# Full attention: the rows of maxima are sent from ScalarE's queue instead of SP's

## The reference, cut to what matters

```
xn  = layernorm(x)                                   # x: 16 x 512 x 256
out = x + full_attention(xn) + two_layers(xn)

full_attention(xn):                                  # 16 heads of 16
    q, k, v = split(xn @ w_qkv.T);  q, k = rope(q), rope(k)
    scores  = q @ k.T / sqrt(16)                     # per head 512 x 512
    out     = softmax(scores) @ v;  return out @ w_out.T
```

## Time and profile before

| | |
|---|---|
| median of 3 runs | 4582.62 us (4575.4 to 4592.76) |
| the profiled execution | 4582.86 us |
| its span | 4581.1 us, 78049 instructions |
| PE busy | 3692.3 us, 81% |
| DVE busy | 2838.8 us, 62% |
| ACT busy | 2356.2 us, 51% |
| POOL busy | 1516.8 us, 33% |
| granted TensorE clock, mean | 0.926 of full speed |
| DMAs of the rows of maxima | 128, 2.0 KB each, from SP |
| stacking DMAs | 384, 64.0 KB each, from SP |

### The profile page before, as it was taken

One profiled execution on the slowest core, in us unless ns is written; L12 is line 12 of the kernel. 1 busy time (PEld: TensorE's weight loads), 2 busy tenths in 40 slices (PEclk: granted clock), 3 DMA queues, 4 the chain that ended last, 5 costly groups with the idle time before them and its releaser, 6 DMA issues.

```text
span 4581.1 us, 78049 instructions
## 1 busy us (share of the span) xinstructions
PE 3692.3 (81%) x28256; PEld 2044.9 (45%) x28256; DVE 2838.8 (62%) x4578; ACT 2356.2 (51%) x2874; POOL 1516.8 (33%) x1468
## 2 busy tenths in 40 slices
PE   3787778777846888888888888666888888888888
PEld 1222222222224555555555555444555555555555
DVE  5676767676734666656666566345566665666664
ACT  1555455555533555555555655334655556555564
POOL 1101111011022434444434444134444344443452
PEclk8999999899967999999999999787999999999999
DMA  2212121212110001000000000200000000000000
GB/s 44 47 38 46 38 47 37 47 37 46 33 62 17 22 21 32 21 21 30 21 27 25 21 30 16 74 17 12 21 30 21 27 26 21 30 21 26 27 21 21
DMA packets 149334, 139.48 MB, mean 30 GB/s; under 512 B 11421, under 2 KB 147665, under 8 KB 149201
## 3 DMA queue, kind: packets, MB, share of 16 engines
q1 hardware_dynamic: 149200, 137.78, 12.0%
HBM read 70.40 MB, written 33.55 MB: 23 GB/s over the span
## 4 chain that ended last, share of the span: by engine, by line
PE 35%; issue 13%; DVE 10%; POOL 9%; ACT 5%; SPq 0%; DMA 0%; POOLq 0%; DVEq 0%; ACTq 0%
PE f_p L950 10%; PE f_p L1056 5%; PE f_p L1020 4%; POOL f_u L1409 4%; POOL f_hT_l L1421 3%; PE f_p L1078 2%; PE f_p L1031 2%; PE f_p L1002 2%; DVE f_negm L1290 2%; DVE f_rt L245 2%; PE f_p L1039 1%; POOL f_qst L1415 1%; PE f_p L934 1%; PE f_p L1046 1%; PE f_p L1006 1%
## 5 line engine op out<-in xcount | busy, mean ns | idle before, releaser
L646 DVE TENSOR_REDUCE m_negm<-m_p 128x2 f16<-128x1024 f32 x512 | 604.9, 1221 | 244.7 <-PE m_p L465 200.7
L565 ACT ACTIVATE m_Pr<-m_p 128x1024 f32<-128x1024 f32 x512 | 492.4, 1018 | 264.6 <-PE m_p L483 264.0
L1404 POOL TENSOR_TENSOR f_u<-f_u,f_bt 128x1024 f32<-128x1024 f32 x128 | 301.5, 2356 | 903.1 <-DVE f_bt L1262 903.1
L1290 DVE TENSOR_REDUCE f_negm<-f_p 128x4 bf16<-128x1024 f32 x256 | 293.5, 1223 | 194.8 <-PE f_p L973 194.5
L685 POOL TENSOR_TENSOR m_rc<-m_rc,m_rs 128x1024 f32<-128x1024 f32 x32 | 75.5, 2359 | 979.6 <-DVE m_rs L641 978.0
L492 PE MATMUL m_o<-m_Pr,m_vm 128*32 128x512 f32 x2048 | 368.1, 672 | 17.2 <-ACT m_Pr L565 16.6
L963 PE MATMUL f_p<-f_ident,f_qst 128*128 128x128 f16 x1024 | 97.3, 251 | 309.8 <-POOL f_qst L1415 309.8
L1421 POOL TENSOR_TENSOR f_hT_l<-f_hp,f_hT_h 128x512 f16<-128x512 f32 x192 | 235.6, 1227 | 308.2 <-ACT f_hp L1184 307.5
L1285 DVE TENSOR_TENSOR f_klt<-f_u,f_khh 128x512 f16<-128x512 f32 x128 | 135.4, 1058 | 317.9 <-ACT f_khh L1131 317.9
L1078 PE MATMUL f_p<-f_xhT_h,f_w_h 128*128 128x512 f16 (+1 forms) x768 | 302.7, 394 | 0.0
L1078 PE MATMUL f_p<-f_xhT_h,f_w_l 128*128 128x512 f16 (+1 forms) x768 | 300.9, 392 | 0.0
(11 more groups left out here) (225 smaller groups left out, 8965.4 us busy)
## 6 DMA issues: line engine op xcount, KB each, us to landing
f_xs<-out SPq DMA_DIRECT2D x32, 512.0 KB, 4.2
f_xr<-out SPq DMA_DIRECT2D x32, 512.0 KB, 3.9
f_ar<-attn_res SPq DMA_DIRECT2D x32, 512.0 KB, 4.4
out<-f_xb SPq DMA_DIRECT2D x32, 512.0 KB, 3.2
m_xin<-in_L_attn_x SPq DMA_DIRECT2D x16, 512.0 KB, 4.3
m_QT<-m_hi SPq DMA_DIRECT2D x128, 64.0 KB
m_KT<-m_hi SPq DMA_DIRECT2D x128, 64.0 KB
out<-m_xn SPq DMA_DIRECT2D x16, 512.0 KB, 6.5
```

Of the source, the lines that this page charges most:

```text
L565: act.activation(Pr[kt % 2][:, 2 * u:2 * u + 2, :].rearrange("p h t -> p (h t)"), psum[w.slot("M2", g, kt, u)][:, :], ACT.Exp).then_inc(*w ...
L646: dve.tensor_reduce(negm[:, t, pr // 2, :, pr % 2], psum[w.slot("M1", h, u)][:, :].rearrange("p (a k) -> p a k", a=2), AX.X, ALU.max, nega ...
L1290: dve.tensor_reduce(negm[:, :, h], psum[w.slot("L1", h)][:, :].rearrange("p (n k) -> p n k", n=NT), AX.X, ALU.max, negate=True).then_inc(* ...
L1404: pool.tensor_tensor(u[t][:], u[t][:], bt[:], ALU.add).then_inc(*bt_used.up(I))
```

## The change

What does not change: the arithmetic, the tiles, the order of TensorE, VectorE and GpSimd, and the places of the four MM steps in ScalarE's list. What changes is who issues the 128 DMAs of the rows and where the other steps of SP stand because of it. In ScalarE's step `mmax`, behind the copy, ScalarE now waits until its own copy has completed (`is_drained`) and issues the two DMAs. The step `mmax` of SP is gone, and so are its four words in SP's list. SP's list begins with two more quotes, so that its first word reads `""B.MM,0`; that stream isn't given, and the word is dropped.

```diff
-        "SP": """B.MM,0 A.LX T.MP B.MM,1 B.MM,2 A.ST,0 A.ST,1 A.ST,2 A.ST,3 A.ST,4 A.ST,5 B.MM,3 A.ST,6 A.ST,7 A.LS""",
+        "SP": """""B.MM,0 A.LX T.MP A.ST,0 A.ST,1 A.ST,2 A.ST,3 A.ST,4 A.ST,5 A.ST,6 A.ST,7 A.LS""",
...
                 act.wait_ge(*mrow_done.at(I, 32 * g))
                 act.activation(mT[:], psum[w.slot("MM", g)][:, :].bitcast(F16)[0:HG, 0:T], ACT.Copy)\
                     .then_inc(*w.frees("MM", g))
+                act.wait_ge(*w.is_drained("MM", g))
+                for e in range(2):
+                    act.dma_start(QT[I.par][e * S + KR:e * S + KR + 1, g * HG // 2:(g + 1) * HG // 2, :],
+                                  mT[e * HG // 2:(e + 1) * HG // 2, :]).then_inc(*mrow_done.up(I, 16))
...
-            def mmax(I, g):
-                hold(w.is_drained("MM", g))
-                for e in range(2):
-                    sp.dma_start(QT[I.par][e * S + KR:e * S + KR + 1, g * HG // 2:(g + 1) * HG // 2, :],
-                                 mT[e * HG // 2:(e + 1) * HG // 2, :]).then_inc(*mrow_done.up(I, 16))
-
...
-            w.run({"LX": lx, "LS": ls, "ST": stack, "MM": mmax, "MP": mp})
+            w.run({"LX": lx, "LS": ls, "ST": stack, "MP": mp})
```

## The result

The kernel after takes 4651.6 us (median of 4 runs, 4645.8 to 4655.6), the one before 4585.2 (4 runs): ratio 1.0145, 95% interval 1.0122 to 1.0168. That is 66 us slower. I had forecast 41, and the time lies 6 us above the range. The profiled execution has a span of 4651.6 us, 70.5 above that of before.

A forecast was written before the change was run, and what follows sets the result against it. A once-per-batch loop through the stacking DMAs' transfers and ScalarE's Exps was taken to bound the attention phase. 22.5 + 3 + 12 + 3.75 = 41 us on about 4583 gave 4624 us, range 4598 to 4646.

The forecast's parts named there:

- The sign: Whole kernel: predicted slower, by 41 us or 0.9%; chance of slower by over 0.5% put at 0.73.
- the first mechanism: ScalarE's wait and two issues behind MM,1's copy delay the Exp that releases XT, so lengthen the batch loop.
- d: What one MM step costs ScalarE, as delay of its next activation: taken as 1.5 us, between 0.2 and 1.85.
- MM,1, 22.5 us: MM,1's issue on ScalarE lies fully on the batch loop, 15 times 1.5 us: 22.5 us.
- the 48.7 us of one batch: Time read from M1,0,0 to the next batch's lo,0 in the kernel before; predicted to become 1.5 us longer.
- MM,2, MM,3 and the queue, 3 us: MO,2 up to 3 us later, mostly covered by the stack before M1,0,0; 3 us put for all batches.
- The third rival: MM,3's rows stay stuck behind the stack on their own queue: 10 us more, 4634; shares the forecast's 0.60.
- The round's end, 12 us: At four hardware-loop round ends, MO,2's 3 us delay goes straight into the loop: 12 us; the least sure term.
- VectorE's 10 us: VectorE's idle of 9.9 to 10.3 us at round ends, read as a fixed jump time counted from MO,2's end.
- The last batch, 3.75 us: In the last batch, where nothing else overlaps, ScalarE's issue costs 3.75 us.
- The fourth rival: Faster: MM,3's rows pass the stack, M2,3 starts up to 3.6 us earlier, TensorE keeps its clock; 4542, chance 0.07.

The follow-up runs named there:

- one experiment: Kernel before, with SP's list reordered: MM,2's rows behind ST,0 and MM,3's behind 15 stacking DMAs; 4604.7 us against 4584.8, ratio 1.0041.
- all but MM,1: Kernel after, but SP sends MM,1's rows, ScalarE those of MM,0, MM,2 and MM,3; 4645.7 us against 4586.3 for the kernel before, ratio 1.0126.
- SP held: Kernel after, but SP waits for MM,3's copy before ST,6, as before, and issues nothing for it; 4627.2 us, 1.0087 over the kernel before.
- ScalarE pays: Kernel before, with an added ScalarE copy into an unread tile behind each MM copy, SP still sending the rows; 4615.2 us against 4584.8, ratio 1.0075.
- MM,2 on ScalarE: Kernel before, but ScalarE alone sends MM,2's rows and SP the others; 4587.5 us against 4590.5, ratio 0.9993.

## Why the prediction was right and wrong

The sign and the first mechanism were right: ScalarE's issue costs what SP's did (d 1.49), and MM,1 stands on the loop. The size was not.

- **MM,1, 22.5 us.** From its copy to XT it is 1.29 us more, 15 times, 19 us. But in the kernel after almost the same is given back ahead of it: M1,0,0 to MM,1's copy is 1.38 us shorter, 21 us. M1,0,0 is so late there that VectorE's jump and most of the low clock (4.5 us before, 1.1 after) are over when it starts. I had taken the 48.7 us of one batch for the mean; it was 50.3.
- **MM,2, MM,3 and the queue, 3 us.** This step failed, in two places: that MM,3's pair in SP's list stops SP for 1.3 us and its removal is worth "nothing", and that the rows land at worst 7.5 us after their issue (4.9 to 10.3, 8.8 on average). The pair was not a cost but a place: it kept the last six stacking DMAs behind the rows. Without it 21.7 instead of 18 are ahead, and the rows land 3.2 us later in each of 15 batches, 48 us. The third rival named the mechanism and priced it at 10, since it didn't count that SP would issue more of the stack ahead of the rows.
- **The round's end, 12 us.** MO,2's delay does reach the loop there, but at TensorE, not VectorE: from the rows' landing to M2,3 it is 18 us over five round ends. MO,2 ends 3.2 to 6.3 us later there, and the jump behind it is itself longer, 3.7 to 9.0 us instead of 0.2 to 3.9, which I had no term for. VectorE's 10 us were not in the way, because M1,0,0 came later than they ended.
- **The last batch, 3.75 us.** From its M1,0,0 to its last M2 it is 3.3 us more.
- **The sum** of what was measured: 15 × (4.41 between lo,0 and M1,0,0, less 0.10 between M1,0,0 and lo,0) = 65, and 3.3 for the last batch: 68 of the 70.5 us of span.
- **The fourth rival** (faster) had the clock the wrong way round, as far as one experiment tells: when M2,3 started early, the low clock came behind M1,0,0, where it counts, and not ahead of it.
- **The total was closer than its parts.** Forecast 41, measured 66: the 22.5 for MM,1 had nearly vanished from the loop, and 48 us had come where I had put 3.

What stays open: whether rows on ScalarE's queue wait at the same place as GpSimd's, on the stack's engines. Their packets start late too, but a pair has only eight, none of which goes early, so they don't tell. Why the jump's length varies from 0.2 to 9 us is open too. The queue for instructions has 102 packets in the five kernels in which all five of TensorE's jumps took 3.5 us or more (after, all but MM,1, SP held, ScalarE pays, and MM,2 on ScalarE), and 66 or 75 in the other kernels with a loop, in which only some did. That fits a reload of the loop's code in every round instead of some, but nothing here shows what decides it.

## What to carry to other kernels

A DMA in an engine's list is also a barrier for what stands behind it. Before moving a small urgent transfer to another engine, count the bulk transfers that will then be issued ahead of it: where the transfers and not the issue set the pace, each cost the small one 0.8 us on average here, and a queue of its own didn't help. And price a step in combination: of the steps moved here, one was worth 27 us alone and about 6 with the others (0 to 22 by the intervals), another 30 alone and 59 together with two that showed no price of their own.

## What the runs showed of the hardware

- Rows of 2 KB issued from ScalarE or GpSimd, on queues of their own, did not land ahead of the 64 KB transfers that SP had issued before: with 20 to 24 of these ahead they landed 4.9 to 10.3 us after issue from ScalarE (mean 8.8) and, with 19 to 23, 6.2 to 9.6 us from GpSimd (mean 8.6), against 2.2 with nothing ahead (ScalarE, MM,1).
- Of GpSimd's packets half went at once and half waited 2.8 us or more, in each of 15 batches.
- ScalarE's issue of a 2 KB DMA took 0.58 us, about the same as SP's (0.57 to 0.63); the wait for its own copy cost 0.03 us.
- GpSimd's pair took 1.05 us, and M1,0,0 to the next lo,0 was not longer for it (49.5 us, before 50.3).
- TensorE's branch back took between 0.2 and 9.0 us in the same loop. VectorE's took 0.06 us, but in four of the five round ends of the kernel before some 10 us passed from its last instruction ahead of it to its first reduction behind it, which kept M1's first tile waiting for 2 us. Written out, the loop ran 10 us (before) and 14 to 18 us (after) faster.
